# Attention scores by query half for a pair of heads, instead of head by head

## What is computed

```
latent_kv = x @ w_kv_down                  # x here is layernorm(x)
k, v = split(latent_kv @ w_kv_up)
q = x @ w_q
att = softmax(causal(q k^T * 64**-0.5))    # per sequence and head, 256 x 256
y = (att @ v) @ w_out
x = x + layernorm(y)
x = x + layernorm(experts(layernorm(x)))
```

## Time and profile before

| | |
|---|---|
| median of 3 runs | 1458.52 us (1456.14 to 1459.41) |
| the profiled execution: span from first to last instruction | 1455.6 us |
| its own time | not listed apart; its span is 2.9 us under the median |
| attention (first T to last T) | 16.1 to 1213.8 us |
| PE busy | 1391.0 us, weight loads 1319.1 us |
| DVE busy | 1244.1 us |
| ACT busy | 1092.1 us |
| POOL busy | 809.9 us |
| granted TensorE clock, mean | 0.982 |

### The profile page before, as it was taken

One profiled execution on the slowest core, in us unless ns is written; L12 is line 12 of the kernel. 1 busy time (PEld: TensorE's weight loads), 2 busy tenths in 40 slices (PEclk: granted clock), 3 DMA queues, 4 the chain that ended last, 5 costly groups with the idle time before them and its releaser, 6 DMA issues.

```text
span 1455.6 us, 37790 instructions
## 1 busy us (share of the span) xinstructions
PE 1391.0 (96%) x10656; PEld 1319.1 (91%) x10656; DVE 1244.1 (85%) x4806; ACT 1092.1 (75%) x3186; POOL 809.9 (56%) x1216
## 2 busy tenths in 40 slices
PE   7999999999999999999999999999999999599993
PEld 6999999999999999999999999999999999488872
DVE  4888898989898989898888989898989887499994
ACT  5888787878787878788787878787878886366661
POOL 3455455555555555555555555555555554178886
PEclk9999999999999999999999999999999999699997
DMA  5000000000000000000000000000000000312120
GB/s 195 5 9 13 12 11 10 10 11 11 12 11 12 11 8 11 12 11 12 11 11 12 11 10 11 10 11 12 11 12 11 9 9 13 96 48 63 58 63 8
DMA packets 38795, 32.42 MB, mean 22 GB/s; under 512 B 4882, under 2 KB 35990, under 8 KB 38304
## 3 DMA queue, kind: packets, MB, share of 16 engines
q1 hardware_dynamic: 31968, 21.61, 4.9%
q0 software_dynamic: 4608, 8.67, 1.7%
q10 hardware_dynamic: 2112, 1.11, 0.3%
HBM read 20.35 MB, written 12.07 MB: 22 GB/s over the span
## 4 chain that ended last, share of the span: by engine, by line
PE 76%; DVE 11%; issue 7%; ACT 2%; POOL 2%; DMA 1%; DVEq 0%; SPq 0%; POOLq 0%; ACTq 0%
PE psS L577 22%; PE psZU L643 11%; PE psP L606 11%; PE psZU L628 11%; PE psZU L631 6%; PE psT L594 4%; PE psT L596 4%; PE psT L595 4%; DVE ff L365 2%; DVE wup_s L382 1%; DVE on L391 1%; DVE nscore L849 1%; POOL out L444 1%; DVE gg L400 1%; DVE p_lo L859 1%
## 5 line engine op out<-in xcount | busy, mean ns | idle before, releaser
L1035 POOL TENSOR_TENSOR prob<-prob,rinv 128x256 f32<-128x256 f32 (+1 forms) x512 | 412.6, 826 | 501.3 <-DVE rinv L830 496.0
L720 ACT ACTIVATE prob<-nscore,nmax 128x128 f32<-128x128 f32 (+1 forms) x1024 | 457.9, 448 | 227.3 <-DVE nmax L849 226.6
L849 DVE CUSTOM_DVE_ANT_0 nscore<-psS,mask 128x128 f32<-128x128 f32 (+1 forms) x1024 | 320.8, 351 | 3.8 <-issue 0.2
L577 PE MATMUL psS<-xt_hi,t_lo 128*128 128x128 f32 (+1 forms) x1024 | 305.5, 298 | 0.0
L577 PE MATMUL psS<-xt_lo,t_hi 128*128 128x128 f32 (+1 forms) x1024 | 284.4, 278 | 0.0
L577 PE MATMUL psS<-xt_hi,t_hi 128*128 128x128 f32 (+1 forms) x1024 | 283.8, 277 | 0.0
L859 DVE TENSOR_TENSOR p_lo<-psP,p_hi 128x768 fp32r<-128x768 f32 x256 | 243.7, 952 | 0.9 <-ACT p_hi L693 0.8
L606 PE MATMUL psP<-ident,prob 128*128 128x128 f32 x1536 | 209.6, 272 | 7.8 <-DVE p_lo L859 7.8
L836 DVE TENSOR_TENSOR t_lo<-psT,t_hi 128x512 fp32r<-128x512 f32 x256 | 175.9, 687 | 44.3 <-ACT t_hi L693 41.6
L693 ACT ACTIVATE p_hi<-psP 128x768 fp32r<-128x768 f32 x256 | 206.1, 805 | 3.3 <-PE psP L606 1.6
L865 DVE TENSOR_TENSOR z_lo<-psZU,z_hi 128x512 fp32r<-128x512 f32 x256 | 176.8, 690 | 31.1 <-ACT z_hi L693 14.6
(11 more groups left out here) (167 smaller groups left out, 3315.4 us busy)
## 6 DMA issues: line engine op xcount, KB each, us to landing
fin<-routed_rows SPq DMA_DIRECT2D x40, 136.0 KB
wx<-ffn_w SPq DMA_DIRECT2D x2, 2058.0 KB, 12.3
xin<-x SPq DMA_DIRECT2D x32, 128.0 KB, 2.1
xres<-x SPq DMA_DIRECT2D x32, 128.0 KB, 2.1
out<-res,fin POOLq DMA_INDIRECT x80
routed_rows<-padr ACTq DMA_DIRECT2D x4, 272.0 KB, 4.8
routed_rows<-padr SPq DMA_DIRECT2D x4, 272.0 KB, 4.2
wup_s<-wup SPq DMA_DIRECT2D x1, 1024.0 KB, 5.0
```

The source lines that it names most:

```text
L577: last = mm(psS[:, h, a:z], tt[:, tb, h, q * P:(q + 1) * P], xx[:, xb, 0:z - a], start=(n == 0), stop=(n == 2))
L720: last = nc.scalar.activation(prob[:, p1, h, a:z], nscore[:, h, a:z], ACT.Exp, bias=nmax[:, p1, h, q:q + 1], scale=-1.0, accum_out=rsum[:, ...
L849: last = v.tensor_tensor_reduce(nscore[:, h, a:z], psS[:, h, a:z], mask[:, a:z], -1.0, -MASKED, ALU.add, ALU.min, nmax[:, p1, h, q:q + 1])
L1035: last = g.tensor_tensor(pr, pr, rinv[:, p2, :, q:q + 1].broadcast_to([P, 2, z - a]), ALU.mult)
```

## The change

The stationary and the moving operand of the scores change places, and the halves of a slot's work are query halves q instead of heads. The key-side matrix of each head is made transposed (`head_matrices`), so that T holds transformed tokens on the key side. For a query half the plain tokens of the half are loaded, and the transformed tokens of both heads move: 2 x 128 columns for q = 0, into one bank, 2 x 256 for q = 1, into the other. `score_max(0)` and `exps(0)` then have two tiles of 128 x 128, one for each head, and `score_max(1)` and `exps(1)` have two of 128 x 256. Semaphores, their counts and the order of each engine's program stay.

```
+QCOLS = ((0, P), (P, 3 * P))
...
+        psQ = (psS[:, 1, 0:T].rearrange("p (h k) -> p h k", h=2), psS[:, 0, :].rearrange("p (h k) -> p h k", h=2))
...
-                    mm(psAB[j % 2][:, e, 0:P], wq_s[h, j, :], kv_t[h, 0, j, :], start=True, stop=True)
+                    mm(psAB[j % 2][:, e, 0:P], kv_t[h, 0, j, :], wq_s[h, j, :], start=True, stop=True)
...
-            def scores(h, tb, xb, freed):
+            def scores(q, tb, xb, freed):
...
-                terms = ((t_lo, xt_hi), (t_hi, xt_lo), (t_hi, xt_hi))
-                for q, (a, z) in enumerate(((0, P), (P, 384))):
-                    for n, (tt, xx) in enumerate(terms):
-                        last = mm(psS[:, h, a:z], tt[:, tb, h, q * P:(q + 1) * P], xx[:, xb, 0:z - a],
-                                  start=(n == 0), stop=(n == 2))
+                nk = (q + 1) * P
+                for n, (xx, tt) in enumerate(((xt_hi, t_lo), (xt_lo, t_hi), (xt_hi, t_hi))):
+                    last = mm(psQ[q], xx[:, xb, q * P:(q + 1) * P], tt[:, tb, :, 0:nk], start=(n == 0), stop=(n == 2))
...
-                    for h in range(2):
-                        scores(h, (s - 1) % 2, xb, 2 * (g0 + s - 2) + 1 + h if live(2) else None)
+                    for q in range(2):
+                        scores(q, (s - 1) % 2, xb, 2 * (g0 + s - 2) + 1 + q if live(2) else None)
...
-                def exps(h):
+                def exps(q):
...
-                    act.wait_ge(S["nmax_ready"], 2 * (g0 + s - 1) + 1 + h)
-                    for q, (a, z) in enumerate(((0, P), (P, 384))):
+                    a, z = QCOLS[q]
+                    act.wait_ge(S["nmax_ready"], 2 * (g0 + s - 1) + 1 + q)
+                    for h in range(2):
...
-                def score_max(h):
+                def score_max(q):
...
-                    wait_apart(dve, S["s_ready"], 2 * (g0 + s - 1) + 1 + h)
-                    for q, (a, z) in enumerate(((0, P), (P, 384))):
-                        last = v.tensor_tensor_reduce(nscore[:, h, a:z], psS[:, h, a:z], mask[:, a:z],
+                    a, z = QCOLS[q]
+                    wait_apart(dve, S["s_ready"], 2 * (g0 + s - 1) + 1 + q)
+                    for h in range(2):
+                        last = v.tensor_tensor_reduce(nscore[:, h, a:z], psQ[q][:, h, :], mask[:, a:z],
```

## The result

The changed kernel takes 1459.76 us (median of 20 runs, 1457.89 to 1461.95) against 1457.97 for the kernel before: ratio 1.0017, 95% interval 1.001 to 1.0023. It is slower by 0.17%, small but clear of the noise, where 1453 was forecast. Three of the 20 runs of the kernel before took 1783 to 2819 us; the other 17 have a median of 1457.25, and the ratio goes by them.

A forecast was written before the change was run, and what follows sets the result against it. PE was taken to bound at 75.0 us an iteration, a DVE-ACT ring close behind at 74.87. The ring becomes 74.87 + 1.42 - 0.87 = 75.42; with the ends -5.4, so 1450.2, plus 2.9: 1453, range 1449 to 1458.

The forecast's parts named there:

- What bounds the kernel now: In the loop PE sets the pace at 75.0 us an iteration, with DVE and ACT's ring almost equal at 74.87.
- the ring: Dependences on DVE and ACT: t_lo, maxima, p_lo, second maxima, second exponentials, t_hi, next t_lo; 4.21 us a plain slot.
- PE, 87 us saved: Score matmuls on PE: 0.34 us less a slot, 5.4 an iteration, 87 over 256 slots, gained if nothing else bound.
- rival 1: PE was the only bound, so the time falls by 87 us to 1371; chance 0.04.
- Maxima: On DVE the first group takes 0.42 us instead of 0.55, the second 0.68 instead of 0.55; zero for the ring.
- hitr: Routing step on DVE: both sequences now pay 0.82 us, counted already in the ring's own 74.87.
- Exponentials: ACT's second group takes 0.98 us instead of 0.90, 0.08 to 0.09 more on the ring; +1.4 over 16 slots.
- z_hi and z_lo: z_hi on ACT ends 0.22 us earlier, z_lo on DVE starts at once; three slots give 3 x 0.29 = 0.87.
- Rival 4: PE's new gaps make the clock fall to 1.2 GHz, each uncovered slot costing 14 x 4.2 = 59: from 1512; chance 0.02.
- Rival 3: The ring is lengthened and nothing given back, as z_hi does not come earlier: +8 us, 1467; chance 0.24.
- The 12 iterations with a branch behind them: Loop iterations from stall to stall: 75.42 us each against 75.54 measured, -1.4 in all.
- The last iteration of the loop: No branch behind it, PE alone bound at 4.48 us a slot and the ring is now 4.29: -0.3.

The follow-up runs named there:

- e1: Changed kernel with its new matmuls kept, but maxima and exponentials taken head by head as in the kernel before; 1445.79 us, ratio 0.9922.
- e10: Kernel before with z_hi alone moved ahead of the first exponentials on ACT; 1461.69 us, ratio 1.0028.
- e6: Changed kernel with GpSimd's split of the next sequence's tokens moved from slot r = 4 to r = 6; 1445.52 us, ratio 0.9917.
- e7: Changed kernel with query half 1 first, z_hi ahead of the first exponentials, and GpSimd's token split at slot r = 6; 1399.4 us, ratio 0.9596.
- e3: Changed kernel with query half 1 taken first and half 0 last, everything else the same; 1462.12 us, ratio 1.0038.

## Why the prediction was wrong

Its picture of the two bounds held, one step of it failed, and its sum missed, sign included: the forecast was the difference of two numbers within 1% of each other. The sizes below set one iteration of the changed kernel against e1, which has its matmuls and the old groups. The forecast step from the one to the other is 1.42 - 0.87 = 0.55 us; 75.88 - 74.86 = 1.02 was measured.

- *What bounds the kernel now.* Right. PE was put at 75.0 an iteration and the ring, without PE, at 74.87: e1 shows 74.78 to 75.06 (one iteration with a fall of the clock aside), and e10 that PE held the kernel before. That the table's iteration of e1 has 74.86 is partly luck.
- *PE, 87 us saved and not passed on.* Right; rival 1 is out. By their starts the scores take 1.14 a slot against 1.46, so 0.32 less where 0.34 was forecast; PE's busy time of an iteration fell by only 3.4 (74.99 to 71.59), not 5.4.
- *Maxima, "zero for the ring", and hitr, "counted in the ring's own 74.87 already".* This step failed. The 0.13 by which p_lo was to start earlier exists in plain slots and not in the two routing slots. I followed hitr, rightly (0.81 in both sequences), and left out oh, two lines on, which meets xk_lo. There the 0.13 that the shorter first maxima give are lost, while the longer second maxima cost theirs in full. I had forecast 5.81 + 0.09 = 5.90; it is 6.03. Against e1 a routing slot is longer by 0.24 to 0.25 instead of 0.09: 0.31 an iteration. e6, which takes xk_lo out of the way, shows the cause.
- *Exponentials.* The mechanism was right and the size off: 0.09 was forecast for a plain slot, with 0.10 as the most, and 0.11 measured (4.20 to 4.31). The pair is 0.51 + 0.49; the 0.51 follows an idle moment of 0.19. Over 11 slots of an iteration this is 0.24.
- *z_hi and z_lo.* Right in mechanism, a little small: slots r = 1 came to 4.44, where the terms give 4.64 or 4.65 less 0.20, and the branch's slot to 6.26, where 6.73 less 0.22 and 0.20 is 6.31. Against e1 the three slots gave 0.71, not 0.60, part of it scatter at the branch: -0.11.
- Together 0.31 + 0.24 - 0.11 = 0.44 of the 0.47 that an iteration missed; the rest is rounding.
- *Rival 4, the clock.* It was given a chance of 0.02 and priced from whole slots at the lower level. A milder form came true, 0.4 to 0.5 us in 4 iterations, 1.8 us. The earlier trace rows showed another gap and no fall, and that was no evidence for this one.
- *Rival 3.* Slower was its outcome, at 1467, but not for its reason: the three z_lo gains came in full.
- *The 12 iterations with a branch behind them.* Forecast -1.4, measured +5.5: the miss of 6.9 is 12 x 0.46 = 5.5, the clock's 1.8 and 0.4 of scatter in the changed kernel's branch slots, less 0.8, since an iteration of the kernel before is 75.61 in the mean and not 75.54.
- *The last iteration of the loop.* Forecast -0.3, measured +0.7. Half of this miss is a slip in my sum: no branch is taken there, so the 0.42 that the branch's slot gains must not be counted. My own terms give +0.2.
- *PE's new waits cost nothing.* Right but for the four falls of the clock.
- *Ends.* The first 32 slots: -2.6 forecast, -2.65 measured (t_lo of slot 32 starts at 162.01 us, before at 164.66). The last slots: -0.8 forecast, -1.1 measured. Drain and the experts' part: -0.3 and -0.3. The median lies 2.1 us above the profiled span, where I had added 2.9.

## What to carry to other kernels

When the busiest engine is at 99%, walk the dependences of the others before cutting its work: here a ring of two engines, 85% and 75% busy, was 0.2% behind PE's busy time, and it took all but 0.8% of a saving of 6%. What is moved within such a ring counts at full price where it lies on it and at nothing beside it. So shorten the last link (the small tiles second) and pull what sits on the second path (z_hi) into a hole: with GpSimd's split moved as well this gave 4%, from moves that add and remove no work. They pay only together with the saving on PE: an iteration of e7 takes 71.9 to 72.2 us, and the old matmuls alone keep PE busy for 75.0; of the three moves, e10 tried z_hi's on the kernel before, and it gave nothing. Last, a sum whose result is smaller than one forgotten small instruction per iteration has no sign.

## What was not expected of the hardware

- DVE's gap at the loop's branch is not a constant. It shrinks from 2.3 us to 1.2 us as the last wait of the iteration is met 1.1 us earlier, with 2.08 and 1.73 in between; in five kernels the next instruction starts 3.0 us after the end of the z_hi that the last wait is for.
- A PE gap of 1.2 to 1.7 us, once in 76 us, let the granted clock fall in some iterations (4 of 13 in the changed kernel and in e3, 2 in e1) and in none of 13 in e6; with 1.4 us of matmuls in it the clock stayed at 1.00 in all 13.
- A DVE instruction on 128 x 16 elements took 174 ns alone and 611 ns beside a GpSimd one.
